# Attention loop on one core: the output product moved ahead of the value products, the layer-norm between the two exponentials, the square behind them

## The reference

```
def attention_sublayer(x, kv, q_w, k_w, v_w, o_w):      # 16 heads of 8 features
    q, k, v = heads(x @ q_w), heads(kv @ k_w), heads(kv @ v_w)
    p = softmax(q @ k.T * 8 ** -0.5 + causal_mask)       # 64 x 64 for each head
    return (p @ v) @ o_w
x = layernorm(x + attention_sublayer(x, x, ...))         # stage 0
x = layernorm(x + attention_sublayer(x, ctx, ...))       # stage 1, keys and values of ctx
h = x + attention_sublayer(rope(rms_norm(x)), ...)       # stage 2
h = h + moe(rms_norm(h))     # 8 experts, the best 2 of each token, silu gate
x = layernorm(x + h)
```

## Time and profile before

| | |
|---|---|
| median of 3 timed executions | 263.25 us |
| profiled execution | 265.62 us, its span 263.7 us |
| busy in the span | PE 195.7, DVE 181.3, POOL 118.9, ACT 116.5 us |
| the attention loop | from about 17 to 143 us of the span |
| one iteration in stages 0 and 1 | 4.79 to 4.90 us |

### The profile page before, as it was taken

The page is one execution under the profiler, slowest core; times in us unless marked ns, Lnnn a source line. Parts: engine busy times, 40 slices in busy tenths (PEclk is TensorE's granted clock), DMA queues, the critical chain, the costliest instruction groups (busy, mean ns, idle before and its releaser), DMA issues. The chain is left out here.

```text
span 263.7 us, 7264 instructions
## 1 busy us (share of the span) xinstructions
PE 195.7 (74%) x2444; PEld 167.5 (64%) x2445; DVE 181.3 (69%) x410; ACT 116.5 (44%) x385; POOL 118.9 (45%) x220
## 2 busy tenths in 40 slices
PE   0489999999999999979864522899999999910000
PEld 0357788888888887857653521799999999900000
DVE  6306888887889999987973487277667776614444
ACT  1335677577577676756442120244444444400000
POOL 0215356556577887642224303435444430037771
PEclk9999999999999999997998555599999999985555
DMA  7699900000008000000000000011122332012112
GB/s 234 155 328 382 270 8 4 2 4 2 4 1 241 3 4 2 4 10 14 22 12 20 11 0 22 22 38 50 50 60 43 53 42 42 22 30 60 50 40 80
DMA packets 21338, 16.08 MB, mean 61 GB/s; under 512 B 3032, under 2 KB 18464, under 8 KB 21312
## 3 DMA queue, kind: packets, MB, share of 16 engines
q1 hardware_dynamic: 19248, 12.02, 15.5%
q0 software_dynamic: 1344, 2.76, 5.2%
q10 hardware_dynamic: 720, 0.95, 1.1%
HBM read 11.78 MB, written 3.93 MB: 60 GB/s over the span
## 5 line engine op out<-in xcount | busy, mean ns | idle before, releaser
L473 POOL DMA_INDIRECT early<-xm_scratch,tok_i x26 | 25.8, 994 | 44.0 <-DMA early<-xm_scratch,tok_i 26.4
L899 DVE TENSOR_REDUCE smax<-score 128x16 f32<-128x1024 f32 x24 | 29.3, 1220 | 15.6 <-PE score L548 13.9
L381 POOL TENSOR_TENSOR k<-kt,cst 128x512 f32<-128x512 f32 x24 | 25.3, 1055 | 21.9 <-ACT kt L773 21.9
L906 DVE TENSOR_TENSOR s_sb<-score,smax 128x1024 f32<-128x1024 f32 x24 | 29.4, 1225 | 1.3 <-DVE smax L899 0.4
L916 DVE RECIPROCAL rsum<-bank 128x128 f32<-128x128 f32 x24 | 22.9, 954 | 6.5 <-PE bank L581 6.2
L783 ACT ACTIVATE pt_sb<-bank 128x512 f32<-128x512 f32 x48 | 26.0, 594 | 2.5 <-PE bank L496 2.0
L548 PE MATMUL score<-k,q 64*128 64x256 f32 x192 | 26.9, 404 | 0.0
L496 PE MATMUL bank<-cst,s_sb 128*128 128x128 f32 x192 | 25.0, 273 | 0.0
L704 PE MATMUL bank<-w,pt_sb 128*128 x160 | 23.2, 288 | 0.0
L496 PEld LDWEIGHTS bank<-cst,s_sb 128*128 128x128 f32 x192 | 21.7, 141 | 0.7 <-issue 0.7
L548 PEld LDWEIGHTS score<-k,q 64*128 64x128 f32 x192 | 20.2, 206 | 2.3
(11 more groups left out here) (166 smaller groups left out, 395.1 us busy)
## 6 DMA issues: line engine op xcount, KB each, us to landing
w_up<-in_L_ffn_W SPq DMA_DIRECT2D x2, 2048.0 KB, 12.7
w<-in_L_ffn_W SPq DMA_DIRECT2D x8, 256.0 KB, 5.9
y_scratch<-eo SPq DMA_DIRECT2D x1, 1536.0 KB, 7.7
y_scratch<-eo SPq DMA_DIRECT2D x10, 128.0 KB
cst<-in_consts ACTq DMA_DIRECT2D x1, 672.5 KB, 4.1
early<-in_x SPq DMA_DIRECT2D x1, 512.0 KB, 5.9
early<-in_ctx SPq DMA_DIRECT2D x1, 512.0 KB, 4.2
xm_scratch<-xm SPq DMA_DIRECT2D x8, 64.0 KB, 1.5
```

The costliest lines, as they stand in the source:

```text
L381: g.tensor_tensor(k2[:, n % 3, :, :, :], kt[:, n % 2, :].rearrange("c (b u k) -> c b u k", b=2, u=1).to_broadcast([P, 2, NQ, S]), mask_p.r ...
L473: pool.indirect_dma_start(xg[:, j, :], None, xm_d[:, :], bass.IndirectOffsetOnAxis(ap=tok_i[:, j:j + 1], axis=0)).then_inc(g_gather, 16)
L899: v.tensor_reduce(smax[:, :, :], score[:, :, :].rearrange("q b (p k) -> q b p k", k=S), AX.X, ALU.max).then_inc(d_mx, 1)
L906: v.tensor_tensor(s_sb[:, :, :].rearrange("q b (p k) -> q (b p) k", k=S), score[:, :, :].rearrange("q b (p k) -> q (b p) k", k=S), smax[:, ...
```

## The change

```
-                if 1 <= it <= STEPS:
-                    values(it - 1)
                 if 2 <= it:
                     out_proj(it - 2)
+                if 1 <= it <= STEPS:
+                    values(it - 1)
...
-                if it - 3 >= 2 * NT:
-                    square(it - 3)
                 if it + 2 < STEPS:
                     copy_xt(it + 2)
                 if 1 <= it <= STEPS:
                     exponent(it - 1, 0)
-                    exponent(it - 1, 1)
                 if 3 <= it < 2 * NT + 3:
                     finish(it - 3)
+                if 1 <= it <= STEPS:
+                    exponent(it - 1, 1)
+                if it - 3 >= 2 * NT:
+                    square(it - 3)
```

More of the change, by code:

```diff
@@ L644, in _ @@
                     project(it + 2)
+                if 2 <= it:
+                    out_proj(it - 2)
                 if 1 <= it <= STEPS:
                     values(it - 1)
-                if 2 <= it:
-                    out_proj(it - 2)
                 if it == STEPS:
```

## The result

The changed kernel took 272.12 us (median of 4, 270.89 to 272.56) against 263.38 for the kernel before (median of 4): ratio 1.0302, 95% interval 1.0227 to 1.0377. Six further executions of it in a later comparison had a median of 272.94 against 265.33 for 11 of before, ratio 1.0304 (1.0246 to 1.0361). It is slower, as forecast, but by 3.0% and not by the 2.0% of 268.4 over 263.25, and 272.12 us lies outside the range of 265.6 to 271.2. The profiled execution took 271.88 us, its span 270.0, against 265.62 and 263.7.

A forecast was written before the change was run, and what follows sets the result against it. TensorE's own work was taken to bound stages 0 and 1; +7.7 us (ring and iteration 2) and -2.6 in stage 2 gave +5.1, carried to the median as 268.4 us, range 265.6 to 271.2.

The forecast's parts named there:

- The ring: Stages 0 and 1: output product waits for the layer-norm, closing a chain over four engines; 5.34 us an iteration instead of 4.86.
- the last iteration: Iteration 18, the last with the wait: no residual product in front, about 0.2 us less, so 5.12 us.
- Iteration 2: Output product, not yet held by a layer-norm, pushes the value products by about 0.30 us.
- Stage 2: From it = 19 to 25, the square no longer stands before xt and the exponentials: -2.6 us, between -1.0 and -3.5.
- The change is taken over unchanged: The +5.1 us for the profiled execution, 2.37 us over the median of 263.25, is added to that median: 268.4 us.
- The 1 us for the clock elsewhere: Behind the loop, the clock's rises may fall otherwise by up to 1 us either way.
- The rope beside the expansion: Rival, stage 1: VectorE's second rope product meets GpSimd's expansion of the keys; +2.9 us, 271.3 us, chance 0.09.
- Faster: Rival: the layer-norm's result is there when the projections end, so the output product is not held; 256.4 us, chance 0.06.
- The clock: Rival: TensorE, idle 0.75 us in each iteration, loses its full clock in stretches; 272.4 us, chance 0.05.
- The account of the layer-norm's place: On ScalarE, the layer-norm ahead of the second exponential gains nothing usable: it can't start before 3.07 us after the reciprocal.

The follow-up runs named there:

- cut: Changed kernel plus a ScalarE copy of bank ps_y into SBUF, which statistics and layer-norm read and the output product awaits; layer-norm behind both exponentials: 258.41 us.
- pe_only: Kernel before with only TensorE's order changed, output product ahead of the value products; ScalarE's order as before: 270.57 us, ratio 1.0231.
- after_link: Changed kernel with one more small GpSimd product in the chain from mean and variance to the layer-norm: 278.6 us, a single execution.
- square_only: Kernel before with only the square moved behind the exponentials (and the layer-norm, which it never meets): 262.08 us, ratio 0.994.
- base2: Kernel before, unchanged, profiled once more to look for an execution of the faster group: 264.45 us.
- norm_only: Kernel before with only the layer-norm moved between the two exponentials; TensorE's order and the square as before: 270.2 us, ratio 1.0235.
- base: Kernel before, unchanged, profiled again to see its executions one by one: 265.66 us.
- after2: Changed kernel, unchanged, profiled again to see whether its slow start varies; median of six executions 272.94 us.

## Why the prediction was wrong

- **The ring: right, and sized nearly right.** The rows of before gave 5.40 us; 5.38 was measured. My step "up to 0.2 us off, so the ring lies between 5.20 and 5.40; I take 5.34" was a discount for overlaps and a shorter change of form that no run shows in the ring: from 595 to 574 are 0.64 us there, against 0.65 in the rows. Only where 595 does not wait is it shorter, 0.54 in cut. With the last iteration, at 5.22 and not 5.12, the section measured +8.10 where the prediction had +7.4: 0.7 us of the miss. The experiments pe_only, after_link and cut show the ring from three sides: its cause alone, a link more, and the link taken away.
- **Iteration 2: right.** +0.32 against +0.3.
- **Stage 2: right in place, wrong in what it was compared with.** -2.6 was forecast for the profiled execution, -2.72 measured. The part of it that I explained with the half clock of the earlier trace rows was there: an execution of before without it takes 28.81 us instead of 30.14, and against that the gain is 1.39. The square's new place is enough for all of it (square_only).
- **"The change is taken over unchanged": the step that failed.** The miss is 3.7 us, from 268.4 to 272.12. In the loop the profiles measured +5.70 where +5.1 was forecast, 0.6 of it. The profiled execution lay 2.37 us over the median of three, and I carried +5.1 over to that median. What can make it longer was in part in my hands: the stretch at half clock of the earlier trace rows, which cost 1.33 us. The start came up to 1.5 later than in base2. The three executions were, by their times, of the kernel's shorter group. No execution of that group was profiled; that it has no half clock in stage 2 is taken from its mean clock (0.893 to 0.898) and from base2. From such executions the removal of the half clock could not be gained a second time; the step should have been +7.0 (8.10 + 0.32 - 1.39), and the time 270.3, still inside the range. The median over more executions, 264.7 to 265.3, shows how small a sample three were.
- **The 1 us for the clock elsewhere: sized too small, and not the clock alone.** "May fall otherwise by up to 1 us either way" stood against the remaining 1.8 us, which carry the time out of the range. By the table of sections the start of the changed kernel came at 27.56 or 26.05 (25.48 in the best profile of before), and the experts took 65.11 or 66.90 us; each of its two profiles has one of the two costs, and each cost comes up in a profile of before as well. That the changed order brings them more often isn't shown. All ten executions of the changed kernel lie above 270.3 (the shortest at 270.89), and 3.6 us of start could be taken away. The cost in the experts' part is not the clock's in base2, where TensorE stood idle at full clock; its cause stays open.
- **The range.** By its own bounds the forecast reached further up: 1.0 us for the ring at 5.40, 1.6 for stage 2 (-1.0 instead of -2.6) and 1.0 for the clock give 272.0. The text allowed stage 2 only 1 us and ended at 270.6, and the range at 271.2.
- **The rivals.** The rope beside the expansion did not meet in the changed kernel, as the two rows had it, but it did in norm_only. The Trainium skill, "SBUF — State Buffer", Who interferes with whom, states that whoever begins first keeps the port; norm_only agrees where the order can be read: rope_b at 86.60, 0.25 us ahead of the expansion at 86.85, took 0.35 us. Where the two began within 0.01 us of each other (both at 81.24; 102.90 and 102.91) the rope took 1.19 to 1.21, even with the earlier start in the trace; these near ties don't decide who was first. Faster was ruled out where it was said to be: the layer-norm is seen 3.58 us after the reciprocal, 0.74 too late. The clock did not fall in the loop in spite of 0.55 us of idle TensorE in each iteration.
- **The account of the layer-norm's place: right.** "Gains nothing it could use": pe_only has the same 5.38.

## What to carry to other kernels

Before an instruction is moved ahead of another on an in-order engine, follow what it waits for back to the last instruction of that engine: if the chain ends at the one that it is moved past, the move closes a ring, and its length is the new iteration, read straight off the rows without a discount. Slack of 0.73 us against a stall of 0.26 does not pay when 1.02 us of cover are given up; free the resource first (here a copy of 0.28 us out of the bank), and the same move gains. And where the profiled execution lies off the timed ones, find out why before a change is carried over.

## What the runs showed of the hardware

- The section of a loop with no clock change repeats to 0.05 us between executions (77.80, 77.76, 77.81; 85.90, 85.91, 85.90), while the whole varies by up to 4.3 us (262.60 to 266.92 for before). The variation sits in three places: the start, the idle stretch of stage 2, and the experts' part.
- Nine products with the identity that nobody reads, put into TensorE's idle times of the first 22 us, made the changed kernel 4.2 us faster in one comparison, of which 2.1 us are the start by the profiles, and the cut one 2.0 us between two (it = 25 at 128.36 instead of 130.36).
- Not settled: the experts' part takes 64.8 to 65.1 us in the profiles of before, base, the changed kernel, pe_only, norm_only and square_only, and 66.7 and 66.9 in base2 and after2, 67.4 in after_link. In after2 the full clock came back 5.4 us after the experts' first product and in the first profile of the changed kernel 3.2 us after it; but in base2 and base after 4.2 and 4.0, so that this can't be the whole cause. In base2 TensorE stands idle for about 1.15 of 50 us at full clock behind that, and in base for none.
- In the start the clock row of the windows reads 1.00 (22 to 24 us in base) also where eight score products took 1.83 us and not 1.04: there the durations must be read beside it.
